# Attention inside a fused conv, scan and attention kernel: score tiles of 64 keys, six key blocks summed on TensorE, raw outputs copied out, and the division moved into the next chunk

## What is computed

```python
qkv = jnp.einsum('bnc,ce->bne', x, W_qkv)
q, k, v = jnp.split(qkv, 3, axis=-1)
q = q.reshape(B, N, HEADS, DIM_HEAD)      # N 4096, HEADS 4, DIM_HEAD 32
k = k.reshape(B, N, HEADS, DIM_HEAD)
v = v.reshape(B, N, HEADS, DIM_HEAD)
q = l2norm_axis1(q)
k = l2norm_axis1(k)
sim = jnp.einsum('bihd,bjhd->bhij', q, k) * SCALE
attn = jax.nn.softmax(sim, axis=-1)
out = jnp.einsum('bhij,bjhd->bhid', attn, v)
```

## Time and profile before

| what | value |
| --- | --- |
| median of 3 runs | 5882.98 us (5876.63 to 5884.37) |
| the profiled execution | 5884.61 us |
| its span | 5882.9 us |
| VectorE busy | 5070.9 us, 86% of the span |
| TensorE matmuls busy | 4708.2 us, 80% |
| ScalarE busy | 3751.1 us, 64% |
| granted TensorE clock, mean | 0.94 of full |

### The profile page before, as it was taken

One profiled execution on the slowest core, in us unless ns is written; L12 is line 12 of the kernel. 1 busy time (PEld: TensorE's weight loads), 2 busy tenths in 40 slices (PEclk: granted clock), 3 DMA queues, 4 the chain that ended last, 5 costly groups with the idle time before them and its releaser, 6 DMA issues. The chain is left out here.

```text
span 5882.9 us, 100771 instructions
## 1 busy us (share of the span) xinstructions
PE 4708.2 (80%) x33880; PEld 1953.7 (33%) x33880; DVE 5070.9 (86%) x6502; ACT 3751.1 (64%) x4897; POOL 1666.3 (28%) x1274
## 2 busy tenths in 40 slices
PE   5776779998777777999867777799986677779997
PEld 3222433333322243333332224333343222433334
DVE  6799779998689977999878997799987899679998
ACT  3666468883466646888346663688924666378882
POOL 1488600000048860000004885000000588500000
PEclk9899989999889998999988999899988899989998
DMA  1000020000000002000000000200000000020000
GB/s 38 0 1 0 15 62 9 9 5 22 22 0 1 0 15 62 9 9 5 22 22 0 1 0 15 62 9 9 5 22 22 0 1 0 15 62 9 9 5 15
DMA packets 41626, 87.14 MB, mean 15 GB/s; under 512 B 11672, under 2 KB 27872, under 8 KB 38112
## 3 DMA queue, kind: packets, MB, share of 16 engines
q1 hardware_dynamic: 41184, 81.11, 5.2%
HBM read 26.55 MB, written 8.39 MB: 6 GB/s over the span
## 5 line engine op out<-in xcount | busy, mean ns | idle before, releaser
L1296 ACT ACTIVATE arena<-ps 128x1024 f32<-128x1024 f32 x2048 | 1912.8, 1027 | 258.9 <-PE ps L1261 241.3
L1311 DVE TENSOR_TENSOR arena<-arena 128x1024 f32<-128x1024 f32 x1664 | 1907.8, 1218 | 35.9 <-ACT arena L1296 30.6
L941 DVE TENSOR_TENSOR_SCAN arena<-ps,hlast,arena 128x512 f32<-128x512 f32 x1024 | 1259.4, 1266 | 5.2 <-DVE arena L923 3.2
L901 POOL TENSOR_TENSOR arena<-arena 128x1024 f32<-128x1024 f32 x512 | 1206.8, 2357 | 25.0 <-issue 2.1
L1261 PE MATMUL ps<-arena 128*32 128x512 f16 x16384 | 1093.4, 383 | 118.2 <-issue 47.2
L1244 PE MATMUL ps<-arena 128*32 128x512 f32 x8192 | 1087.4, 609 | 46.0 <-DVE arena L1316 38.1
L870 ACT ACTIVATE ps<-arena,amat 128x512 f32<-128x512 f32 x1024 | 691.9, 688 | 505.1 <-DVE arena L941 504.3
L838 PE MATMUL ps<-arena,ident 128*128 128x512 f32 x2048 | 980.3, 602 | 7.7 <-POOL arena L901 7.7
L1261 PEld LDWEIGHTS ps<-arena 128*32 128x32 f16 x16384 | 470.7, 97 | 975.3 <-issue 650.9
L1619 POOL MEMSET arena<- 128x1024 f32 x4 | 3.8, 956 | 2694.4 <-POOLq L101 2694.4
L923 DVE TENSOR_TENSOR arena<-arena,ps 128x1024 f32<-128x1024 f32 x512 | 611.2, 1194 | 53.8 <-PE ps L846 53.8
(11 more groups left out here) (245 smaller groups left out, 4387.5 us busy)
## 6 DMA issues: line engine op xcount, KB each, us to landing
arena<-x SPq DMA_DIRECT2D x32, 512.0 KB, 5.4
arena<-arena SPq DMA_DIRECT2D x64, 256.0 KB, 6.0
arena<-arena SPq DMA_DIRECT2D x64, 224.0 KB, 5.8
arena<-arena SPq DMA_DIRECT2D x28, 512.0 KB, 3.5
arena<-pe SPq DMA_DIRECT2D x256, 32.0 KB, 1.8
out<-arena SPq DMA_DIRECT2D x8, 1024.0 KB, 3.9
expw<-L_ffn_expert_w SPq DMA_DIRECT2D x1, 512.0 KB
wqkv<-L_attn_W_qkv SPq DMA_DIRECT2D x1, 192.0 KB
```

What stands on the lines that cost most here:

```text
L901: pool.tensor_tensor(halves(g[s % 4]), halves(hb[s % 4]), cs[s % 4].unsqueeze(1).broadcast_to([128, HD, CH]), ALU.mult).then_inc(hc_s, 1)
L941: dve.tensor_tensor_scan(halves(hb[s % 4])[:, h, :], da(s, h), halves(dbx[s % 2])[:, h, :], k.hlast[:, s, h, :], ALU.mult, ALU.add).then_i ...
L1296: act.activation(probs[p % 8], k.bank(2 * group[p], 2 * CH), ACT.Exp, scale=SCALE / SPLIT ** 2).then_inc(exp_s, 1)
L1311: dve.tensor_tensor(acc[p % 2], acc[p % 2], probs[p % 8], ALU.add).then_inc(acc_s, 1)
```

## The change

Four things in `attend`. The score matmuls of a pair become four of 64 keys, two side by side, instead of eight of 32. `direct` is every fifth block (5, 10, ... 30, six of them) instead of every sixth (5, 11, ... 29, five). ScalarE copies bank O raw into the output tensor after exponential 2 of the next chunk, and VectorE divides that copy in place after its sixth pair of the next chunk, so that reciprocal and product stand amid the next chunk's additions; the weighing of block 0 waits for the copy, and the first sum by ones for the reciprocal. `finish` moves from pair 2 to pair 4. VectorE's sums have two sets of buffers, used in turn, and its loop, like TensorE's, now spans two chunks; ScalarE's first chunk stands ahead of its loop.

```diff
-    acc = [k.at(SUM_AT + i * 2 * CH, 2 * CH) for i in range(2)]
+    sums = [[k.at(at + i * 2 * CH, 2 * CH) for i in range(2)] for at in (SUM_AT, QH_AT)]
...
-    direct = [j for j in range(NJ) if j % 6 == 5]
+    direct = list(range(5, NJ, 5))
...
+    def first(c):
+        return isinstance(c, int) and c == 0
...
         def weigh(c, j):
             pe.wait_ge(exp_s, c * NPAIR + (2 * j + 2 + 3))
-            if j == 0:
-                pe.wait_ge(norm_s, c + 1)
+            if j == 0 and not first(c):
+                pe.wait_ge(o_s, c)
+            if j == direct[0] and not first(c):
+                pe.wait_ge(l_s, c)
...
-                        for t in range(4):
-                            last = pe.matmul(k.ps[32 * t:32 * t + 32, (2 * group[p] + e) * CH:(2 * group[p] + e + 1) * CH],
-                                             ks[:, h, j * 128 + 32 * t:j * 128 + 32 * t + 32], queries[:, h, :],
-                                             start=True, stop=True, tile_position=(0, 32 * t))
+                        for t in range(2):
+                            last = pe.matmul(k.ps[64 * t:64 * t + 64, (2 * group[p] + e) * CH:(2 * group[p] + e + 1) * CH],
+                                             ks[:, h, j * 128 + 64 * t:j * 128 + 64 * t + 64], queries[:, h, :],
+                                             start=True, stop=True, tile_position=(0, 64 * t))
                     last.then_inc(s_mm, 1)
 
-                    if p == 1 and not first:
+                    if p == 1 and not first(c):
                         weigh(c - 1, NJ - 1)
-                    if p == 2 and not first:
-                        finish(c - 1)
+                    if p == 4 and not first(c):
+                        finish(c - 1, 1 - q)
...
     def scalar(act):
-        act.sem_inc(exp_s, 3)
-        k.ready_table(act, ACT.Exp, 1)
-        with act.Fori(0, NCH) as c:
+        def keep_output(c):
+            act.wait_ge(pv_s, c * NJ + (NJ + 4))
+            act.activation(ao[:, cols_of(c)], k.bank(O), ACT.Copy).then_inc(o_s, 1)
+
+        def body(c):
             for p in range(NPAIR):
                 act.wait_ge(s_mm, c * NPAIR + (p + 1))
                 act.wait_ge(pv_s, c * NJ + (p // 2 + 1))
                 act.wait_ge(acc_s, summed(c, p - 8))
                 act.activation(probs[p % 8], k.bank(2 * group[p], 2 * CH), ACT.Exp, scale=SCALE / SPLIT ** 2).then_inc(exp_s, 1)
+                if p == 2 and not first(c):
+                    keep_output(c - 1)
...
     def vector(dve):
-        dve.sem_inc(pv_s, 4)
-        dve.sem_inc(acc_s, NA)
-        dve.sem_inc(norm_s, 1)
-        with dve.Fori(0, NCH) as c:
+        def divide(c):
+            dve.wait_ge(l_mm, c + 1)
+            dve.reciprocal(rl, k.bank(LS)).then_inc(l_s, 1)
+            dve.wait_ge(l_s, c + 1)
+            dve.wait_ge(o_s, c + 1)
+            dve.tensor_tensor(ao[:, cols_of(c)], ao[:, cols_of(c)], rl, ALU.mult).then_inc(norm_s, 1)
+
+        def body(c, q):
+            acc = sums[q]
             for p in range(NPAIR):
...
+                if p == 5 and not first(c):
+                    divide(c - 1)
```

More of the change, by code:

```diff
@@ L1210, in attend @@
     probs = [k.at(8192 + i * 2 * CH, 2 * CH) for i in range(8)]
-    acc = [k.at(SUM_AT + i * 2 * CH, 2 * CH) for i in range(2)]
+    sums = [[k.at(at + i * 2 * CH, 2 * CH) for i in range(2)] for at in (SUM_AT, QH_AT)]
     rl = k.at(RL_AT, CH)
     NJ, NPAIR = L // 128, 2 * (L // 128)
-    s_mm, exp_s, pv_s, acc_s, l_mm, l_s, norm_s = (k.sem(n) for n in (
-        "scores_mm", "probs_ready", "pv_mm", "probs_summed", "sums_mm", "sums_inverse", "chunk_normed"))
+    s_mm, exp_s, pv_s, acc_s, l_mm, l_s, o_s, norm_s = (k.sem(n) for n in (
+        "scores_mm", "probs_ready", "pv_mm", "probs_summed", "sums_mm", "sums_inverse", "output_kept", "chunk_normed"))
     O, LS = 6, 7
     group = [p % 3 for p in range(NPAIR - 1)] + [1]
-    direct = [j for j in range(NJ) if j % 6 == 5]
+    direct = list(range(5, NJ, 5))
     NA = NPAIR - 2 * len(direct)
+    def first(c):
+        return isinstance(c, int) and c == 0
     def summed(c, p):
@@ L1247, in weigh, with finish, body @@
             last.then_inc(pv_s, 1)
-        def finish(c):
+        def finish(c, q):
             pe.wait_ge(acc_s, summed(c, NPAIR - 1))
-            ones_by(acc, False, True).then_inc(l_mm, 1)
-        def body(c, queries, first):
+            ones_by(sums[q], False, True).then_inc(l_mm, 1)
+        def body(c, q, queries):
             for j in range(NJ):
@@ L1277, in staged @@
             pe.wait_ge(staged_s[i], n * 16)
-            body(c, q_now[i], False)
-        body(0, qs[:, :, 0:CH], True)
+            body(c, i, q_now[i])
+        body(0, 0, qs[:, :, 0:CH])
         with pe.Fori(0, NCH // 2 - 1) as cc:
@@ L1285, in tensor @@
         weigh(NCH - 1, NJ - 1)
-        finish(NCH - 1)
+        finish(NCH - 1, (NCH - 1) % 2)
     def scalar(act):
-        act.sem_inc(exp_s, 3)
-        k.ready_table(act, ACT.Exp, 1)
-        with act.Fori(0, NCH) as c:
+        def keep_output(c):
+            act.wait_ge(pv_s, c * NJ + (NJ + 4))
+            act.activation(ao[:, cols_of(c)], k.bank(O), ACT.Copy).then_inc(o_s, 1)
+        def body(c):
             for p in range(NPAIR):
@@ L1296, in scalar @@
                 act.activation(probs[p % 8], k.bank(2 * group[p], 2 * CH), ACT.Exp, scale=SCALE / SPLIT ** 2).then_inc(exp_s, 1)
-    def vector(dve):
-        dve.sem_inc(pv_s, 4)
-        dve.sem_inc(acc_s, NA)
-        dve.sem_inc(norm_s, 1)
-        with dve.Fori(0, NCH) as c:
+                if p == 2 and not first(c):
+                    keep_output(c - 1)
+        act.sem_inc(exp_s, 3)
+        k.ready_table(act, ACT.Exp, 1)
+        body(0)
+        with act.Fori(1, NCH) as c:
+            body(c)
+        keep_output(NCH - 1)
+    def vector(dve):
+        def divide(c):
[6 more added lines that the diff above has]
+            acc = sums[q]
             for p in range(NPAIR):
@@ L1311, in vector @@
                     dve.tensor_tensor(acc[p % 2], acc[p % 2], probs[p % 8], ALU.add).then_inc(acc_s, 1)
[L1312 to L1316, removed]
+                if p == 5 and not first(c):
+                    divide(c - 1)
+        dve.sem_inc(pv_s, 4)
+        dve.sem_inc(acc_s, NA)
+        body(0, 0)
+        with dve.Fori(0, NCH // 2 - 1) as cc:
+            body(cc * 2 + 1, 1)
+            body(cc * 2 + 2, 0)
+        body(NCH - 1, 1)
+        divide(NCH - 1)
     return tensor, scalar, vector
```

## The result

The changed kernel takes 5994.48 us (median of 4 runs, 5988.29 to 5997.33) against 5879.81 us for the one before (4 runs, 5876.56 to 5884.37). The ratio is 1.0192, with a 95% interval from 1.0176 to 1.0208: 115 us slower. The forecast was 5975 us, slower, because TensorE would pay for changing its tile width. The profiled execution took 5988.29 us with a span of 5986.6, 103.7 more than that of before.

What follows compares the result with a forecast made beforehand. TensorE, ScalarE and VectorE were within 10% of each other; two width switches a block make TensorE the bound. Chunks +110.1, loop ends 17.6 for 13.9, slow starts -22.4 give +91.4: 5975 us, range 5825 to 6060.

Steps and rivals of the forecast that it cites:

- the first rival: TensorE between scores and weighing: no drain from 64 to 32 columns, ScalarE stays the bound, 5836 us; chance 0.20.
- the 0.08: Cost in us of one width switch between scores and weighing, below which the change was to come out faster.
- Into the weighing: Width switch from scores to weighing in each block: 0.10 of drain plus 0.03 of exposed load, 0.13 us.
- into the scores: Width switch from weighing to scores in each block: 0.10 of drain plus 0.02 to 0.03 of load, 0.12 us.
- The head: Start of a chunk, first score pair to block 5: 10.5 of work and 1.1 of waiting, 11.5 us.
- The loop end: Where TensorE's loop closes, twice in each batch: full 2.2 us as TensorE is the bound, 17.6 for 13.9.
- rival A: No drain from 64 to 32 columns: chunk 65.7 us, -47 in all, 5836 us; chance 0.20.
- Slow starts: First weighings of a chunk at TensorE's lower clock after the division wait: 22.4 us, taken off as gone.
- The division amid the additions: VectorE's division moved into the next chunk, 4.3 us: costed at nothing, up to 4.3 a chunk without cover.
- B: Only part of the drain, 0.073 to 0.087 us a switch: within 12 us of 5883; chance 0.06.
- C: The two score tiles of 64 don't run abreast: 27 us a chunk more, about 6850 us; chance 0.02.
- D: VectorE's division stalls the ring of exponentials: at most 4.3 us a chunk, mostly hidden; no chance of its own.

Runs made afterwards that it cites:

- Both probes: Kernel before plus a tiny 64-column matmul ahead of the first score pair of a block, or ahead of both: 5990.1 us and 6182.75 us.
- the halves: Changed kernel with each weighing from block 5 on cut in two, one half behind each score pair: 6903.7 us; with 32-key tiles 5856.67 us.

## Why the prediction was right

*The bound and the sign.* "TensorE becomes the bound" and a block of 1.97 us are what the profile shows (1.98, TensorE busy for 69.69 of 70.45). The forecast rested on rows of the convolution with widths of 128 and 32; that 64 against 32 costs the same was open, and was the first rival. Both probes and the tiles alone settle it: 0.11 to 0.12 us for each change with the probes, 0.13 with the tiles, above the 0.08 from which the sign was to turn. The rule of the Trainium skill (TensorEngine Tiling (Array Packing), Key Properties) that a changed tiling mode drains TensorE holds for 64 and 32 columns as well. That it is a drain is shown by the loads, which never run ahead across a change and do so by 0.43 without one, and by the halves, which stopped overlapping.

*The terms.* Into the weighing I took 0.13 (0.12 measured), into the scores 0.12 (0.14). The head was 11.5 (11.44). The chunk was 69.9 and is 70.45: 27 blocks of 1.98 with six direct sums of 0.86 make 58.6 for 58.4, and the last pair of a chunk, which waits for an exponential, starts 0.4 late, which I had left out. That is 0.55 a chunk, up to 18 us. The span of the profiled execution is 103.7 us longer where the sum had 91.4. The median is 19.5 us over the forecast; the medians are 115 apart and the profiled executions 104, since the one of before (5884.61) lies above all of its four timed runs and the one of the changed kernel is the fastest of its four.

*The loop end* was to cost the full 2.2 as nothing hides it, which is about right. The changed kernel, TensorE at such a place:

```profile
1030.67 1.05 PE L1266 MATMUL ps<-arena 128*64 128x512 f16 x8 [1.92 <-issue]
```

The chunk with it is 72.43, 1.98 over the plain one; the seven other such chunks have 2.1 to 4.3 more, all eight together 21.1 us for the 17.6 of the sum.

*The rest of the change*, forecast as a gain of 47 us if it stood alone (rival A), is one of 30 us against its own reference. The chunk is 66.07 where I had 65.7, and loop ends there cost about 1.9 instead of 1.73. Slow starts did not all go: two chunks have one.

*The division amid the additions* cost nothing that shows: with tiles of 64 TensorE sets the pace, and at 32 columns the five-block kernel, which has the copy, the moved division and the later closing sums together, is 57 us faster. No run has one of these three alone. Rivals B, C and D are out: no change of width was cheaper than 0.10, score tiles of 64 run abreast (0.43 a pair), and the exponentials do not queue behind the division: in the first batch's attention they waited 5.4 us for additions in all, 3.2 in the kernel before. Two slips of the prediction are small: B's 17 us for each 0.01 counts the 54 changes in the 27 blocks and leaves out the 8 of the head, which would make it about 20; and the chances of the list add up to 0.22 for faster and 0.72 for slower, where 0.23 and 0.71 are given.

*What stays open:* what decides whether a chunk's first weighings run at the lower clock. These slow starts went or grew rarer in the kernels with the 64-wide score tiles and in that with six direct blocks, and some remained with five. The wait alone does not explain them, though I had put them down to it: the kernel with the score tiles alone still waits 1.22 us for the division, that with six direct blocks 1.27 us, and each has two slow starts left. That the 22.4 us which I took off were nearly all gone is thus partly luck.

## What to carry to other kernels

Matmuls that alternate closely on TensorE should have one tile width; here each change of width cost 0.10 to 0.14 us, twice in a loop of 1.86 us, whichever width was the wider and however little stood between. A bundle of edits is worth taking apart: the copy, the moved division and the later closing sums were a gain that the tiles hid, the sixth direct block gave part of it back, and the kernel with five direct blocks and tiles of 32 is 1.0% faster than the one before. Where three engines are within 10% of each other, an edit that adds nothing to any engine's work can still choose which of them bounds.

## What was unexpected of the hardware

Work in different column tiles overlaps even where it belongs to different groups of matmuls, scores and weighing: with all tiles 32 wide, a weighing cut in two halves of 0.86 us each cost 12 us in all, since scores filled the free tiles; with a change of width between, the same cut cost 909 us, some 700 of them lost overlap. And fewer columns did not load faster: 128 float16 columns took 98 ns, 64 took 109 and 32 took 97.
